# First stage of an attention and expert layer: rows normalised by VectorE, one f16 product for the keys' bias, other places for the setup's loads

## The chip, the cores and the metric

One core of one Trainium2 chip (trn2) runs the whole program. The metric is the device time of one execution in microseconds; the median of the runs counts. The profile is one further execution, taken by the hardware profiler.

## What is computed

The reference takes x of shape (2, 2048, 512) in f32, normalises each row over its 512 values, and gives x + attention(xn) + experts(xn):

```python
xn = _layernorm(x, axis=-1)
# attention, 16 heads of 32, latent size L = 128
c = jnp.einsum('bhsd,hld->bhsl', xh, Wdkv)
c = (c - mu) * jax.lax.rsqrt(var + 1e-05)
c = c * ln_g[None, :, None, :] + ln_b[None, :, None, :]
scores = jnp.einsum('bhsl,bhtl->bhst', q_lat, c) * (1.0 / np.sqrt(L))
w = jax.nn.softmax(where(mask, scores, -inf), axis=-1)
# experts: 8, the two with the highest gate logits, mean of relu(xn @ w + b)
x = x + attention(xn) + experts(xn)
```

The latent rows c are never formed. Since they are linear in a head's 32 values up to their scale, the setup folds `Wdkv`, `Wuk`, `Wuv`, `ln_g` and `ln_b` into 32x32 matrices per head. The variance of c comes from a quadratic form, keys and values from products of `xn * rs`, where `rs` is one over the deviation of c per row and head. The part of the keys that `ln_b` gives is a constant vector, the keys' bias.

## The kernel before

The program has four stages: setup with folding; the first stage, which makes queries, keys, values, gate logits and the f16 pieces of the normalised rows and stores them in DRAM; the attention per head; the experts and the last projection. The change touches the setup and the first stage.

The first stage works on 32 tiles of 128 rows, in chunks of four (CT = 4), the chunks of the two batches in turn, so eight chunks. Each engine has its own instruction list, in an order written out by hand, and waits on semaphores. In step p the tile at p gets its keys and values, the tile at p + 2 (QUERIES_AHEAD) its variance, queries and gate logits, the tile at p + 3 (TURN_AHEAD) is turned, and the tile at p + 4 (ROWS_AHEAD) is normalised. Statistics are read three tiles further ahead still (`means`, L785, L792). `run_tiles` (L264 to L273) runs the steps, four of them ahead of tile 0. Per step:

- **GpSimd** normalises the tile at p + 4 (L507: `(x - mean) * rs4`), subtracts its f16 half (L510, `xl_done`), and multiplies the tile at p + 2 by `rs` (L516, `xr_done`).
- **ScalarE** copies the turned `xr` of tile p (L666), makes the f16 half of the tile at p + 4 (L673, waits for `xn_done`), the queries' f16 half (L679), copies the turned tile p + 3 (L686), takes a square root (L693), makes the keys' f16 half (L699) and the values (L703). Once per chunk it takes the root of the four row variances (`spread`, L658).
- **VectorE** makes `rs4` once per chunk (L854), then `prod` and `var` for tile p + 2 (L861, L866), the queries' lower half (L868), the keys' lower half of tile p (L876), `rs` of tile p + 2 (L883), once per chunk the gates (L889 to L903), and then one or two row statistics (L785); none in one step of the four, and after the two of a chunk's end their means (L792).
- **TensorE** turns `xr` of tile p (L1095), forms the quadratic form (L1106), queries (L1112) and gate logits (L1119) of tile p + 2, turns tile p + 3 (L1130), and makes keys (L1139, L1140) and values (L1145) of tile p.
- **SP** issues all loads and stores of the stage. In the step of a chunk's tile 3 it waits for the keys' lower half (L379), stores keys, values (L383), rows (L390) and queries (L398), and in the next step loads x for the chunk after next into the same buffer (L372).

The keys' group is one f32 product and one f16 product with the bias for each of four blocks of 128 columns:

```python
t.matmul(PS[:, 5, k * P:(k + 1) * P], bdk[:, k, :], xrT[tl % 2][:, k, :], start=True, stop=False)
last = t.matmul(PS[:, 5, k * P:(k + 1) * P], bk_hl[0:HD + 1, k * P:(k + 1) * P], ones2[0:HD + 1, :],
                start=False, stop=True)
```

In the setup ScalarE issues the small loads and that of `expert_b` to all partitions (L643), waits for it, scales it by 1/2 (L646), and then copies the turned `Wo` (L651), from which TensorE makes the combined output matrix (L1077). VectorE reads the statistics of the first chunk (L785) and then takes the folded matrices out of PSUM (L815 to L821, `fold_done`, for which L1077 waits too), and goes on to the output matrix's lower half (L841) and the first `rs4` (L854).

## Time and profile before

| | |
|---|---|
| median of 3 runs | 1820.91 us (1818.5 to 1821.28) |
| profiled execution | 1804.26 us, its span 1802.5 us |
| busy: TensorE, VectorE, ScalarE, GpSimd | 1658.1, 1143.8, 969.2, 680.2 us |
| first normalisation starts | 49.84 us |
| last lower half of the keys ends | 290.5 us |
| first scores of the attention | 306.18 us |

The rows below are from the profiled execution; times are microseconds from the span's start unless marked ns. In a timeline a row is one instruction, or several of one kind in a row (x4), with start, duration, engine, line, operation, output and inputs with shapes; in brackets the time that the engine was idle before it and what ended that. A start with SPq or ACTq is a transfer being issued. PEclk is the granted share of TensorE's clock of 2.4 GHz. In these rows `arena` stands for many buffers: x, the normalised rows, queries, keys and values all lie in it.

### The profile page before, as it was taken

The page shows a single profiled execution, that of the slowest core. Times are in us where ns is not written, and L with a number is a line of the kernel's source. Part 1 is how long each engine was busy: PE and PEld are TensorE (multiplying, and loading weights), DVE is VectorE, ACT ScalarE, POOL GpSimd, SP SyncE. Part 2 cuts the span into 40 slices and gives each one's busy share as a digit, 9 for nine tenths or more (in the row PEclk, how much of TensorE's full clock was granted, in tenths as well). Part 3 has the DMA queues.
Part 4 walks back from the last instruction along what each step waited for, and adds up shares of the span by engine and source line. Part 5 has one row for each costly group of instructions (what it writes and reads, how often), then busy time and mean ns, then how long its engine had stood idle before and what let it go on. Part 6 is the DMA issues. An engine that isn't in the chain of part 4 may idle for free.

```text
span 1802.5 us, 46334 instructions
## 1 busy us (share of the span) xinstructions
PE 1658.1 (92%) x13408; PEld 940.8 (52%) x13409; DVE 1143.8 (63%) x2524; ACT 969.2 (54%) x1788; POOL 680.2 (38%) x1036
## 2 busy tenths in 40 slices
PE   4689885999999999999999999999999899998776
PEld 2567774455555555555555555555555355554333
DVE  3455556777777777777777777777777244444555
ACT  2455552566666666666666666666666533333332
POOL 1556550588222222322322322322222333332554
PEclk8899897899999999999999999999999899999998
DMA  5255645021020111111111112012111155554776
GB/s 144 94 172 181 186 142 166 8 61 30 30 59 29 29 49 39 29 37 51 29 29 59 29 29 59 29 29 59 29 29 36 55 173 174 170 174 148 234 236 221
DMA packets 126984, 160.87 MB, mean 89 GB/s; under 512 B 28352, under 2 KB 77504, under 8 KB 126816
## 3 DMA queue, kind: packets, MB, share of 16 engines
q1 hardware_dynamic: 108336, 121.15, 21.8%
q0 software_dynamic: 12992, 35.77, 7.2%
q10 hardware_dynamic: 5616, 3.45, 0.6%
q8 instruction: 21, 0.34, 0.1%
q14 instruction: 19, 0.16, 0.0%
HBM read 99.03 MB, written 61.15 MB: 89 GB/s over the span
## 4 chain that ended last, share of the span: by engine, by line
PE 68%; issue 8%; POOL 8%; DVE 8%; DMA 5%; ACT 2%; DVEq 0%; ACTq 0%; POOLq 0%; SPq 0%
PE PS L1213 26%; PE PS L1160 25%; PE PS L1264 10%; DMA arena<-expert_rows,cur 4%; POOL arena L507 4%; PE PS L1225 3%; DVE pm L971 3%; PE PS L1246 2%; POOL token_of_place L528 1%; POOL arena L510 1%; DVE arena L1034 1%; DMA eb_bc<-in_expert_b 1%; DVE arena L1035 1%; POOL arena L627 0%; ACT arena L686 0%
## 5 line engine op out<-in xcount | busy, mean ns | idle before, releaser
L971 DVE TENSOR_REDUCE pm<-PS 128x1 f32<-128x512 f32 (+3 forms) x1280 | 732.0, 603 | 279.9 <-PE PS L1160 273.3
L1160 PE MATMUL PS<-arena 96*64 96x512 f16 (+7 forms) x5120 | 723.0, 354 | 29.0 <-DVE PS L964 14.8
L726 ACT ACTIVATE arena<-PS 128x512 f32<-128x512 f32 (+1 forms) x1152 | 607.5, 574 | 258.5 <-PE PS L1160 255.1
L1213 PE MATMUL PS<-arena 128*33 128x512 f32 (+3 forms) x2560 | 660.1, 532 | 0.7 <-POOL arena L539 0.7
L1160 PEld LDWEIGHTS PS<-arena 96*64 96x64 f16 (+1 forms) x5120 | 354.4, 110 | 352.3 <-issue 141.5
L539 POOL TENSOR_SCALAR_AFFINE_SELECT arena<-arena 128x256 f32<-128x256 f32 (+1 forms) x256 | 111.0, 434 | 403.0 <-ACT arena L726 399.6
L1213 PEld LDWEIGHTS PS<-arena 128*33 128x33 f32 x2560 | 173.7, 112 | 83.7 <-POOL arena L539 2.8
L1160 PE MATMUL PS<-later,deny 128*64 128x128 f16 x1024 | 175.1, 223 | 0.0
L1264 PE MATMUL PS<-w_hi,arena 128*128 x576 | 172.9, 382 | 0.3 <-issue 0.3
L743 ACT ACTIVATE arena<-PS 128x1024 f16<-128x1024 f32 x72 | 73.7, 1024 | 151.3 <-PE PS L1246 151.3
L554 POOL TENSOR_TENSOR arena<-bv_bc,rden 128x128 f32 (+1 forms) x128 | 51.1, 399 | 236.5 <-DVE rden L984 236.0
L1011 DVE SCALAR_TENSOR_TENSOR arena<-PS,eb_bc 128x512 f32<-128x512 f32 x72 | 49.8, 692 | 127.8 <-PE PS L1264 127.8
L1160 PEld LDWEIGHTS PS<-later,deny 128*64 128x64 f16 x1024 | 92.5, 112 | 51.8 <-issue 24.8
L1264 PE MATMUL PS<-w_lo,arena 128*128 x288 | 110.0, 382 | 0.0
L719 ACT ACTIVATE turn<-PS 128x264 f32<-128x264 f32 x128 | 49.9, 390 | 102.4 <-PE PS L1225 102.4
L1296 PE MATMUL PS<-comb_hl,arena 128*128 128x512 f16 x384 | 96.5, 406 | 0.4 <-ACT arena L761 0.4
L547 POOL TENSOR_TENSOR bv_bc<-turn 128x132 f32<-128x132 f32 x128 | 53.1, 415 | 105.1 <-ACT turn L719 105.0
L733 ACT ACTIVATE arena<-PS 97x512 f32<-97x512 f32 x128 | 76.5, 598 | 27.6 <-PE PS L1213 27.6
L507 POOL TENSOR_SCALAR arena<-arena,mv,rs 128x512 f32<-128x512 f32 x32 | 66.3, 2073 | 51.9 <-DVE rs L854 51.9
L761 ACT ACTIVATE arena<-PS 128x1024 f16<-128x1024 f32 x32 | 32.8, 1024 | 96.1 <-PE PS L1283 96.1
L627 POOL DMA_INDIRECT arena<-expert_rows,cur x64 | 67.7, 1058 | 36.4 <-POOL cur L622 26.0
L1264 PEld LDWEIGHTS PS<-w_hi,arena 128*128 128x128 f16 x576 | 53.6, 98 | 52.7 <-issue 2.2
(177 smaller groups left out, 1690.0 us busy)
## 6 DMA issues: line engine op xcount, KB each, us to landing
expert_rows<-arena SPq DMA_DIRECT2D x72, 256.0 KB, 2.0
arena<-q_pieces SPq DMA_DIRECT2D x96, 128.0 KB
arena<-k_pieces SPq DMA_DIRECT2D x96, 128.0 KB
v_rows<-arena SPq DMA_DIRECT2D x8, 1056.0 KB, 6.4
arena<-v_rows SPq DMA_DIRECT2D x32, 264.0 KB
arena<-in_x SPq DMA_DIRECT2D x8, 1024.0 KB, 7.3
xn_rows<-arena SPq DMA_DIRECT2D x16, 512.0 KB, 4.3
q_pieces<-arena SPq DMA_DIRECT2D x32, 256.0 KB, 4.5
```

The lines of the kernel that those rows point to most:

```text
L507: g.tensor_scalar(xn[:, tl, :], x_in[u][:, tl, :], mv[:, u, tl, 0:1], rs4[:, u, tl:tl + 1], ALU.subtract, ALU.mult).then_inc(s["xn_done"], 1)
L539: g.affine_select(out=both[:, :, 0:wm], in_=both[:, :, 0:wm], compare_op=ALU.is_ge, fill=nought, base=0, pattern=[[step, 2], [1, wm]], cha ...
L627: g.indirect_dma_start(out=y_g[u][k], out_offset=None, in_=y_dram, in_offset=bass.IndirectOffsetOnAxis(ap=cur[:, TOP * u + k:TOP * u + k + ...
L726: a.activation(probs[kk % 4][:, a_ * CH:a_ * CH + w], PS[:, s2_bank(k, x), 0:w], ACT.Exp, scale=SCALE).then_inc(s["exp_done"], 1)
L733: a.activation(ot[q % 2][0:2 * HD + V1, :], PS[0:2 * HD + V1, 6 + q % 2, :], ACT.Copy).then_inc(s["ot_done"], 1)
L743: a.activation(xg_T[u].rearrange("p z k c -> p (z k c)"), PS[:, 4 + 2 * u:6 + 2 * u, :].rearrange("p z c -> p (z c)"), ACT.Copy).then_inc( ...
L971: v.reduce_max(pm[:, c, r, p:p + 1], PS[:, S1_BANK[n], 0:w], AX).then_inc(s["s1_done"], 1)
L1160: last = t.matmul(PS[h:h + P // 2, bank, cols], lhsT[:, h:h + P // 2], rhs, start=start, stop=stop)
L1213: last = t.matmul(PS[rows_, 6 + c % 2, CH - wds[a]:CH], v_sb[pu % 2][:, j + a, :], probs[pk % 4][:, a * off:a * off + wds[a]], start=p_ in ...
L1225: last = t.transpose(PS[:, 6 + q % 2, r * P:r * P + W_], ot[q % 2][0:W_, r * P:(r + 1) * P], ident[0:W_, 0:W_])
L1264: last = t.matmul(PS[:, u, :], xg_T[u][:, z, k, :], w[:, ds(e, 1), k * E:(k + 1) * E].rearrange("p e c -> p (e c)"), start=q_ == 0, stop=q ...
L1296: last = t.matmul(PS[:, u, :], oT[u][:, z, k, :], comb_hl[:, y, k, :], start=q_ == 0, stop=q_ == len(terms) - 1)
```

## The change

Three things change. VectorE instead of GpSimd normalises the rows, ahead of `prod` in each step, and the means no longer wait for the rows of the chunk before. The keys' bias is one f16 product of 512 columns, issued before the four f32 products; its operands are 98 rows high, with each block's two halves of the bias at partitions 0, 32, 64 and 96, and a matrix of ones and zeros that picks them. In the setup the load of `expert_b` is issued behind the output matrix's copies and has a semaphore of its own, its scaling comes after the first stage, and the means of the first chunk come behind the folding.

```diff
 # GpSimd, step
                 at = ahead_tile(i, p, ROWS_AHEAD, more)
                 if at:
                     n, u, tl, ii = at
-                    if tl == 0:
-                        pool.wait_ge(s["rs4_done"], count(ii * B + u + 1))
-                    pool.wait_ge(s["xr_done"], count(n - CT + 1))
-                    pool.sem_inc(s["row_from"], 1)
-                    g.tensor_scalar(xn[:, tl, :], x_in[u][:, tl, :], mv[:, u, tl, 0:1], rs4[:, u, tl:tl + 1],
-                                    ALU.subtract, ALU.mult).then_inc(s["xn_done"], 1)
                     pool.wait_ge(s["xh_done"], count(n + 1))
 # ScalarE
-            act.dma_start(eb_bc[:], expert_b.partition_broadcast(P)).then_inc(s["bias_in"], 16)
-            act.wait_ge(s["bias_in"], count(32))
-
-            a.activation(eb_bc[:].rearrange("p e c -> p (e c)"), eb_bc[:].rearrange("p e c -> p (e c)"), ACT.Copy,
-                         scale=1.0 / TOP).then_inc(s["eb_done"], 1)
-
...
+            act.dma_start(eb_bc[:], expert_b.partition_broadcast(P)).then_inc(s["eb_in"], 16)
             spread(0, 0)
             run_tiles(act, step)
+
+            act.wait_ge(s["eb_in"], count(16))
+            a.activation(eb_bc[:].rearrange("p e c -> p (e c)"), eb_bc[:].rearrange("p e c -> p (e c)"), ACT.Copy,
+                         scale=1.0 / TOP).then_inc(s["eb_done"], 1)
 # VectorE, means and setup
                 v.drain()
-                dve.wait_ge(s["xn_done"], count((ii * B + u - 1) * CT))
-                dve.sem_inc(s["aggr_at"], 1)
                 for t in range(CT):
...
-            means(0, 0, range(CT))
             dve.wait_ge(s["fold_ps"], count(1))
...
-            link(v.tensor_copy(bk_hl[0:HD + 1, :], PS[0:HD + 1, 4, :]))
-            link(v.tensor_tensor(bk_hl[HD:HD + 1, :], PS[HD:HD + 1, 4, :], bk_hl[HD:HD + 1, :], ALU.subtract))
-            link(v.memset(ones2[:], 0.0))
-            for r in (0, HD):
-                v.memset(ones2[r:r + 1, :], 1.0)
+            v.memset(bk_rows, 0.0)
+            link(v.memset(bk_pick, 0.0))
+            for k in range(KB):
+                r, c = slice(P // KB * k, P // KB * k + 2), slice(P * k, P * (k + 1))
+                v.memset(bk_pick[r, c], 1.0)
+                link(v.tensor_copy(bk_rows[r, :], PS[r, 4, c]))
+                r = slice(P // KB * k, P // KB * k + 1)
+                v.tensor_tensor(bk_rows[r, :], PS[r, 4, c], bk_rows[r, :], ALU.subtract)
             v.tensor_copy(bv_bc[:], PS[:, 5, :]).then_inc(s["fold_done"], 1)
 
+            means(0, 0, range(CT))
 # VectorE, step
                 if at and at[2] == 0:
                     n, u, tl, ii = at
+                    lnk, cnt = linker(dve, s["dve_rows"], ii * B + u)
                     dve.wait_ge(s["sd4_done"], count(ii * B + u + 1))
-                    v.reciprocal(rs4[:, u, :], sd4[:]).then_inc(s["rs4_done"], 1)
+                    lnk(v.reciprocal(rs4[:, u, :], sd4[:]))
+                if at:
+                    n, u, tl, ii = at
+                    dve.wait_ge(s["xr_done"], count(n - CT + 1))
+                    v.tensor_scalar(xn[:, tl, :], x_in[u][:, tl, :], mv[:, u, tl, 0:1], rs4[:, u, tl:tl + 1],
+                                    ALU.subtract, ALU.mult).then_inc(s["xn_done"], 1)
 # TensorE, step
+                    pe.wait_ge(s["kl_done"], count(n))
+                    R_ = P - P // KB + 2
+                    t.matmul(PS[:, 5, :], bk_rows[0:R_, :], bk_pick[0:R_, :], start=True, stop=False)
                     pe.wait_ge(s["xrt_done"], count(n + 1))
-                    pe.wait_ge(s["kl_done"], count(n))
                     for k in range(KB):
-                        t.matmul(PS[:, 5, k * P:(k + 1) * P], bdk[:, k, :], xrT[tl % 2][:, k, :], start=True, stop=False)
-                        last = t.matmul(PS[:, 5, k * P:(k + 1) * P], bk_hl[0:HD + 1, k * P:(k + 1) * P], ones2[0:HD + 1, :],
-                                        start=False, stop=True)
+                        last = t.matmul(PS[:, 5, k * P:(k + 1) * P], bdk[:, k, :], xrT[tl % 2][:, k, :], start=False, stop=k == KB - 1)
```

What moves on VectorE shows best in the step behind the gates, in the loop of the first stage. Before, one statistic (of a tile seven ahead) is followed at once by `prod`, the product with the quadratic form (waits `y_ps` from TensorE):

```order
L785 BN_STATS stats<-arena 128x6 [waits x_in0]
L859 REGISTER_ALU
L861 TENSOR_TENSOR arena<-PS,arena 128x512 [waits sd_done,y_ps]
L866 TENSOR_REDUCE var<-arena 128x16 [waits prod_done]
L868 SCALAR_TENSOR_TENSOR arena<-PS,arena 128x4x128 [waits qh_done]
L876 TENSOR_TENSOR arena<-PS,arena 128x4x128 [waits kh_done]
L883 RECIPROCAL rs<-sd 128x16 [waits xr_done,sd_done]
```

In the changed kernel the same stretch of VectorE has the normalisation between them:

```order
L778 BN_STATS stats<-arena 128x6 [waits x_in0]
L853 TENSOR_SCALAR arena<-arena,mv,rs 128x512 [waits xr_done]
L859 REGISTER_ALU
L861 TENSOR_TENSOR arena<-PS,arena 128x512 [waits sd_done,y_ps]
L866 TENSOR_REDUCE var<-arena 128x16 [waits prod_done]
L868 SCALAR_TENSOR_TENSOR arena<-PS,arena 128x4x128 [waits qh_done]
L876 TENSOR_TENSOR arena<-PS,arena 128x4x128 [waits kh_done]
L883 RECIPROCAL rs<-sd 128x16 [waits xr_done,sd_done]
```

The normalisation stands behind a statistic that waits for a load of x, and ahead of `prod`, `var` and both lower halves.

At a chunk's border the changed VectorE has this, from `rs` to the normalisation of the next chunk's first tile (the ISA rows are the sequencer's):

```order
L883 RECIPROCAL rs<-sd 128x16 [waits xr_done,sd_done]
L778 BN_STATS stats<-arena 128x6 x2
L783 BN_AGGR mv<-stats 128x2 x4
L848 ISA
L849 RECIPROCAL rs<-sd 128x4 [waits sd4_done]
L852 ISA [waits dve_rows]
L853 TENSOR_SCALAR arena<-arena,mv,rs 128x512 [waits xr_done]
```

The means have no wait for `xn_done` any more, and the normalisation waits for VectorE's own `rs4`.

## Rows read from the trace of the kernel before

**Rows 1.** Chain that ended last, to 420 us: start, duration, what
```profile
49.84 2.08 POOL arena L507
...
71.13 2.07 POOL arena L507
...
245.51 2.07 POOL arena L507
```

**Rows 2.** Timeline of one tile's ring, and the stage's last lower half
```profile
143.13 2.07 POOL L507 TENSOR_SCALAR arena<-arena,mv,rs 128x512 f32<-128x512 f32 x1
...
145.23 0.63 ACT L673 ACTIVATE arena<-arena 128x512 f16<-128x512 f32 x1 [2.51 <-POOL arena L507]
...
148.59 0.24 DVE L883 RECIPROCAL rs<-sd 128x16 f32<-128x16 f32 x1
...
148.91 1.05 POOL L516 TENSOR_TENSOR arena<-arena,rs 128x512 f32<-128x512 f32 x1 [1.80 <-DVE rs L883]
...
289.84 0.69 DVE L876 TENSOR_TENSOR arena<-PS,arena 128x512 f16<-128x512 f32 x1 [3.95 <-ACT arena L699]
```

**Rows 3.** Timeline of TensorE, one step: keys' group, values' group, next turn, next keys
```profile
138.17 0.44 PE L1139 MATMUL PS<-arena 128*128 128x128 f32 x2
...
140.43 1.16 PE L1145 MATMUL PS<-arena 128*128 128x128 f32 x8
141.43 0.60 PE L1095 MATMUL PS<-ident,arena 128*128 128x128 f32 x4
...
143.85 0.44 PE L1139 MATMUL PS<-arena 128*128 128x128 f32 x2
```

**Rows 4.** Groups of instructions by form: count | busy us, mean ns | idle before
```profile
L1296 PE MATMUL PS<-comb_hl,arena 128*128 128x512 f16 x384 | 96.5, 406 | 0.4 <-ACT arena L761 0.4
...
L828 DVE TENSOR_SCALAR arena<-arena 128x512 f32<-128x512 f32 x1 | 0.4, 416 | 0.0
```

**Rows 5.** Timeline of VectorE between `rs` and `prod`, border and gates
```profile
126.20 0.24 DVE L883 RECIPROCAL rs<-sd 128x16 f32<-128x16 f32 x1
...
128.79 0.69 DVE L861 TENSOR_TENSOR arena<-PS,arena 128x512 f32<-128x512 f32 x1
...
141.78 0.24 DVE L883 RECIPROCAL rs<-sd 128x16 f32<-128x16 f32 x1
...
144.35 0.70 DVE L785 BATCH_NORM_STATS2 stats<-arena 128x6 f32<-128x512 f32 x1
144.96 0.68 DVE L861 TENSOR_TENSOR arena<-PS,arena 128x512 f32<-128x512 f32 x1
```

**Rows 6.** Timeline of the attention, where VectorE and GpSimd meet
```profile
345.64 1.05 POOL L564 TENSOR_TENSOR w_hi<-x_g,ws_col 128x512 f16<-128x512 f32 x1
...
346.21 0.51 DVE L976 TENSOR_SCALAR mx<-mx 128x4 f16<-128x4 f32 x1
```

**Rows 7.** Timeline of SP at a chunk's border: keys' stores, load of x
```profile
126.31 0.92 SPq L379 DMA_DIRECT2D k_pieces<-arena  x2
...
133.73 0.61 SPq L372 DMA_DIRECT2D arena<-in_x  x1
```

**Rows 8.** Line L372, the six loads of x in the stage
```profile
DMA to landing us min/median/max: 5.7/7.0/7.5
```

**Rows 9.** Timeline of the setup
```profile
19.35 0.39 PE L1065 MATMUL PS<-arena 128*128 128x128 f32 x2
...
23.86 3.62 ACT L646 ACTIVATE eb_bc<-eb_bc 128x4096 f32<-128x4096 f32 x1 [12.09 <-DMA eb_bc<-in_expert_b]
...
26.94 2.47 DVE L785 BATCH_NORM_STATS2 stats<-arena 128x6 f32<-128x512 f32 x4 [11.12 <-DMA arena<-in_x]
...
29.89 3.55 DVE L815 TENSOR_SCALAR arena<-PS 32x128 f32<-32x128 f32 x12
...
49.40 0.18 DVE L854 RECIPROCAL rs<-sd 128x4 f32<-128x4 f32 x1
```

**Rows 10.** Stretch of 5 us: busy us per engine (instructions), PEclk, DMA share, GB/s
```profile
130.00:135.00 5.00, 5.00 (x20) 3.97 (x20) 1.75 (x4) 2.76 (x6) 2.34 (x3) 0.51 1.05 317
```

More of the change, by code:

```diff
@@ L72, in layer_kernel @@
         ident16 = sb("ident16", [P, P], f16)
-        ones2 = sb("ones2", [HD + 1, P], f16)
         gw_hl = sb("gw_hl", [P, KB, 2, NE], f16)
@@ L127, in layer_kernel @@
         q_hi, q_lo, k_hi, k_lo = (tA(KB * CH, f16).rearrange("p (k s) -> p k s", k=KB) for _ in range(4))
-        bk_hl = tA(E, f16)
         v_st = [tA(CT * H * V1).rearrange("p (h t f) -> p h t f", t=CT, h=H) for _ in range(2)]
+        bk_rows = tA(P, f16)
+        bk_pick = tA(KB * P, f16)
         tA = carve(arena1)
@@ L192, in layer_kernel @@
         s = {n: sem(n) for n in (
-            "eb_done w_in wqo_in g_in wo_in gate_in bias_in boc_done bob_ps bob_done zeroed consts wc_ps wc_done gw_done fold_ps fold_done bk_ps bk_done bv_ps bv_done "
+            "eb_in eb_done w_in wqo_in g_in wo_in gate_in bias_in boc_done bob_ps bob_done zeroed consts wc_ps wc_done gw_done fold_ps fold_done bk_ps bk_done bv_ps bv_done "
             "wot_ps wot_done comb_ps comb_hi comb_done gates_done dve0 "
-            "bd_done x_in0 x_in1 stage_in scaled stage_free pool_link mv_done sd4_done rs4_done xn_done xh_done xl_done tp_ps "
-            "row_from aggr_at xt_done y_ps q_ps g_ps prod_done var_done sd_done rs_done xr_done tr2_ps xrt_done qh_done ql_done "
+            "bd_done x_in0 x_in1 stage_in scaled stage_free pool_link mv_done sd4_done xn_done xh_done xl_done tp_ps "
+            "xt_done y_ps q_ps g_ps prod_done var_done sd_done rs_done xr_done tr2_ps xrt_done qh_done ql_done "
             "k_ps kh_done kl_done vv_ps v_done lg_done dve_rows dve_gates x_out0 x_out1 q_out0 q_out1 k_out0 k_out1 v_out0 v_out1 "
@@ L832, in _ @@
             v.tensor_tensor(bdq_hl[:, 1], bdq, bdq_hl[:, 0], ALU.subtract).then_inc(s["bd_done"], 1)
-            dve.wait_ge(s["bias_in"], count(32))
+            dve.wait_ge(s["bias_in"], count(16))
             link(v.tensor_scalar(bo_bc[:], bo_bc[:], 1.0 / TOP, None, ALU.mult))
```

## The prediction

> **What bounds the kernel now.** All of the change lies before 291 us, in the setup and the first stage, so I read the chain of waits there first: it gives the pace. The first row tile is normalised (L507) at 49.84 us, that of the second chunk at 71.13, that of the eighth and last at 245.51, and the last lower key half (L876) ends at 290.5 [rows 1, 2]. Six chunks of four tiles take 174.4 us, 29.1 each; what comes before the first of them takes 21.3, what follows the last 45.0. The timeline of one tile shows why it is not faster [rows 2]: a ring that runs through four engines. GpSimd normalises a tile (2.07 us from 143.13), ScalarE had stood idle for it 2.51 us and starts the f16 half at 145.23; behind that in ScalarE's fixed order are the queries' half, the turned tile, the square root and the keys' half; VectorE then makes the keys' lower half and at 148.59 the reciprocal `rs`; GpSimd scales with it (1.05 us from 148.91), and only then normalises the next tile. That is 6.81 us a tile at best. TensorE is no part of it but is near: its step is 5.68 us at full clock, of which the keys' group takes 2.26 and the values' 1.00 [rows 3].
>
> **Normalisation on VectorE.** GpSimd loses 32 instructions of 2.07 us, and L516 no longer has one behind it. VectorE gets 32. No row has a TENSOR_SCALAR with two per-partition operands there. The nearest, L828, same shape and f32 from SBUF, takes 0.42 us [rows 4]; the upper bound is 0.69, what the other 512-column instructions of VectorE take (L876 [rows 2]). I take 0.42.
>
> The new ring, piece by piece. From the end of normalisation to the start of `rs`: 145.20 to 148.59, 3.39 us [rows 2]. From `rs` to the next normalisation VectorE does, in its fixed order, one of four things [rows 5]:
> - tile with nothing between: at most the 0.24 of `rs`; VectorE's instructions overlap a little (the statistic of 144.35 is shown with 0.70, and the next starts after 0.61), so I take 0.16;
> - one row statistic: 0.16 + 0.56, 0.72 (0.56 for 0.61, an estimate);
> - two statistics, their means, ScalarE's root, `rs4`: 126.20 to 128.79, 2.6;
> - the gates and one statistic: 141.78 to 144.96, 3.2.
>
> A chunk has each once: 4 x (3.39 + 0.42) + 0.16 + 0.72 + 2.6 + 3.2 = 21.9 us (0.2 more with the longer values). The wait of the means for the previous chunk's rows falls away and costs nothing either way: VectorE has issued those itself.
>
> **GpSimd and VectorE in each other's way.** The trace has a case: L976, a TENSOR_SCALAR out of SBUF, with four elements a partition, takes 0.51 us, more than L828 with 512, when it starts at 346.21 beside L564 of GpSimd, and it ends at 346.72, just behind GpSimd's 346.69 [rows 6]. So a normalisation that meets a GpSimd instruction will end 0.03 to 0.45 us behind it; I take 0.3, since the start of an instruction passes in the shadow as that of L976 did, and its data don't. After `rs` (0.24) GpSimd starts its 1.05 at once; with one statistic between, VectorE comes to the normalisation while it runs, and ends at 0.24 + 0.08 + 1.05 + 0.3 = 1.67 after `rs` instead of 1.14: +0.5. In the other three cases GpSimd has finished or VectorE is first. Chunk: 22.4. The Trainium skill (SBUF - State Buffer, Who interferes with whom) says that a VectorE instruction in a two-port mode and a GpSimd instruction exclude each other for their whole length; by it the whole 0.42 would follow, 0.1 us more per chunk. The rows show less, and I keep the rows.
>
> **The x load.** Here a cover goes. SP stores keys, values, rows and queries and only then issues the load of the chunk after next: 126.31 for the keys of tile 3, 133.73 for the load, so 7.4 us later, and it lands 5.7 to 7.5 us on, 7.0 in the middle [rows 7, 8]. Data are there 14.4 us (13.1 to 14.9) after the keys' lower half of tile 3. Their first statistic runs just ahead of the `prod` at 144.96, from about 144.4, 18 us after it, so nothing waits now. In the new ring it would come due after 2.6 + 0.42 + 3.39 + 0.16 + 0.42 + 3.39 + 2.6 (3.2 less the statistic) - 0.1 = 12.9 us. VectorE then waits 1.5 us for it, and the chunk takes 23.9. Of the six intervals five have such a load behind them: 6 x 22.4 + 5 x 1.5 = 141.9, against 174.4: **-32.5**. The bounds: no wait and no meeting with GpSimd, 6 x 21.9, is -43; at 14.9 -30.
>
> **The bias product.** Four f16 products between the f32 ones go, one of 512 columns comes. The values' group, four f32 pairs of the same shape with nothing between, takes 1.00 [rows 3]; the 512-column f16 product is nearest to L1296, 96.5 us for 384, 0.25 each [rows 4]. Keys' group 1.25 instead of 2.26, TensorE's step 4.67, 18.7 a chunk, below 23.9. So within the chunks it is worth nothing; at the end, where no rows are normalised and the steps follow TensorE, it counts.
>
> **Before and after the six chunks.** Lead-in, 21.3 now: the first three tiles are normalised in one go instead of 4 us apart, so I let the first `prod` come 3 us earlier, at 6 for 9 (an estimate). From there some 3.4 to `rs`, then 0.72 + 0.42 + 3.39 + 2.6: 10.5 and 6 are 16.5: **-5**. End, 45.0 now: three normalised tiles at 6.81 or more (20.6) become 3.97, 6.4 (gates) and 3.97, 14.3, -6.3; the four remaining steps each lose 1.0 of the keys' group: together **-10**.
>
> **Setup.** Today ScalarE stands waiting for `expert_b` until 23.86 and scales it for 3.6 us before it copies the turned `Wo`, and VectorE waits for x before the folding: L815 starts at 29.89, while its products end at 19.74 [rows 9]. Both waits go. The folding starts 9.9 earlier; its small instructions grow: four times a memset, a cast and a subtraction of 128 columns, estimated by L815's 0.28 (3.55 for 12 of 128 columns) and 0.17 for a memset as 3.7 in all against 2.1, so +1.6. What follows, up to `rs4` at 49.40, comes 8.3 earlier: **-8.3**. The means of the first chunk now stand behind the folding, at 28; x landed at 27 with `expert_b` ahead of it, so they don't wait, and end before TensorE's next products do. The load of `expert_b` (2 MB) now runs at 36 us beside nothing, its scaling at the stage's end, where ScalarE's next work is the first softmax, behind the routing of VectorE and the first scores. I cost both at nothing; without that cover it would be 3.6 us.
>
> **Sum:** -8.3 - 5 - 32.5 - 10 = -56. The profiled execution took 1804.3 us (span 1802.5), so 1748 for one like it. It was 0.9% below the median of the runs; the forecast for the median is 1820.9 - 56 = **1765 us**. The later stages only start earlier.
>
> **The rivals.**
> - *Everything hidden fits (18%).* The load lands in 12.9 us, since the transfers wait less for each other, or VectorE is never held. For it: the load alone needs 5.7 to 7.5. Against: SP issues the stores first and the burst stays as large. Chunk 21.9: 11 us less, 1754.
> - *TensorE's clock becomes the bound (22%).* After the wait at a chunk's border the granted clock is 0.51, at the 1.2 GHz level, through 130 to 135 us [rows 10]. Now that hits nobody. A chunk is 18.7 of work at full clock; one such stretch of about 5.7 us adds 2.85, the border's wait 2.2: 23.8, just what I forecast. Two stretches give 26.6, 2.7 x 6 = 16 more: 1781.
> - *Less comes of it (11%).* The normalisation takes 0.69, the f32 products stay at the 0.44 us a pair that they have between the f16 ones [rows 3], or the setup has another wait: up to 10 more, 1775. It is also the case in which the change doesn't do what it says: if a pair costs that without the f16 ones, the keys' group is 1.9 and only 0.3 is saved.
> - *Slower (2%).* The x load decides: each microsecond that it lands later costs 5, since VectorE holds back `prod` and through it everything. From 14.4 + 56 / 5 = 25.6 us the gain is gone. At 28, should the stores of the faster chunk pile up on one queue, +12: 1833. Against it: the one load issued behind a whole burst lands 7.0 us later and the next burst begins only at tile 1, with the load long down.
> - *As forecast (47%).* 1757 to 1773.
>
> **The numbers.** The range takes the fast rival, the forecast and most of the TensorE one: 1750 to 1784. About 0.2% is what a measurement can tell here, 3.6 us. Only the last rival and some unseen wait in a later stage reach that: faster 0.96, same 0.015, slower 0.025.
>
> **What would show it.** The chain from tile to tile runs over VectorE, ScalarE and TensorE with no L507 of GpSimd; chunks of about 24 us; a VectorE wait for the x load of 1 to 2 us per chunk, on the first statistic; normalisations of 0.42 us, about 0.9 where L516's successor runs; the keys' group in 1.25 us; `rs4` first at 41 us. I am wrong on the mechanism if statistics never wait for x, or if TensorE has no idle time at the border; wrong on the size if chunks take under 22 or over 26 us. That stage two starts 56 us earlier and nothing else moves is the last test.

## The result and the profile after

| | before | changed kernel |
|---|---|---|
| median of the runs | 1821.10 us (1818.5 to 1823.49, 4 runs) | 1763.25 us (1759.39 to 1766.15, 4 runs) |
| ratio, with its 95% interval | | 0.9681 [0.9658, 0.9705] |
| profiled execution | 1804.26 us, span 1802.5 | 1764.17 us, span 1762.0 |
| first normalisation starts | 49.84 us | 41.11 us |
| first normalisations of chunks 1 and 2 apart (lead-in) | 21.3 us | 16.2 us |
| the six chunks that follow | 174.4 us, 29.1 each | 143.4 us, 23.9 each |
| from the last chunk's first normalisation to the last lower key half | 45.0 us | 32.3 us |
| last lower key half ends | 290.5 us | 233.0 us |
| first scores | 306.18 us | 248.66 us |
| busy: TensorE, VectorE, ScalarE, GpSimd | as in the table ahead | 1613.6, 1161.9, 967.6, 614.9 us |

So 57.8 us less, against a forecast of 56. The stage itself ends 57.5 us earlier; the two spans are only 40.5 apart, since heads 0 to 3 of the attention took longer in the second execution (75, 35, 35 and 33 us in the one, 81, 39, 41 and 34 in the other, counted from the stage's end to the start of GpSimd's last product of each head, L554 before and L548 after; everything behind them agrees within 0.4). Both kernels have that difference, as the runs below show: it goes with the batch of runs (the three batches below ran on three chips). Comparisons here are therefore between kernels of one batch, or of the first stage alone, which ended within 0.4 us in the three profiles in which it is that of the kernel before (290.53, 290.85 and, on the third chip, 290.80).

One chunk of the changed kernel, from the timeline of VectorE, GpSimd, SP and TensorE (start, duration, engine, line, operation, output and inputs with shapes; in brackets the idle time and what ended it). It answers to [rows 2, 5, 7]:

```profile
119.96 0.24 DVE L883 RECIPROCAL rs<-sd 128x16 f32<-128x16 f32 x1
120.12 0.63 DVE L778 BATCH_NORM_STATS2 stats<-arena 128x6 f32<-128x512 f32 x1
120.28 1.05 POOL L510 TENSOR_TENSOR arena<-arena,rs 128x512 f32<-128x512 f32 x1 [1.81 <-DVE rs L883]
120.67 0.94 DVE L853 TENSOR_SCALAR arena<-arena,mv,rs 128x512 f32<-128x512 f32 x1
...
124.38 0.69 DVE L876 TENSOR_TENSOR arena<-PS,arena 128x512 f16<-128x512 f32 x1 [0.86 <-ACT arena L687]
124.99 0.24 DVE L883 RECIPROCAL rs<-sd 128x16 f32<-128x16 f32 x1
125.10 0.92 SPq L379 DMA_DIRECT2D k_pieces<-arena  x2
...
127.57 0.55 DVE L853 TENSOR_SCALAR arena<-arena,mv,rs 128x512 f32<-128x512 f32 x1
127.75 1.16 PE L1141 MATMUL PS<-arena 128*128 128x128 f32 x8 [1.65 <-ACT arena L654]
...
131.66 0.24 DVE L883 RECIPROCAL rs<-sd 128x16 f32<-128x16 f32 x1
131.82 0.46 DVE L853 TENSOR_SCALAR arena<-arena,mv,rs 128x512 f32<-128x512 f32 x1
131.98 1.20 POOL L510 TENSOR_TENSOR arena<-arena,rs 128x512 f32<-128x512 f32 x1 [1.81 <-DVE rs L883]
132.08 1.13 SPq L372 DMA_DIRECT2D arena<-in_x  x1
...
135.79 0.24 DVE L883 RECIPROCAL rs<-sd 128x16 f32<-128x16 f32 x1
...
139.37 0.69 DVE L778 BATCH_NORM_STATS2 stats<-arena 128x6 f32<-128x512 f32 x1 [1.14 <-DMA arena<-in_x]
139.97 0.53 DVE L853 TENSOR_SCALAR arena<-arena,mv,rs 128x512 f32<-128x512 f32 x1
```

The ring can be walked down these rows. From `rs` at 119.96 over the statistic to the normalisation's end, 1.65 us (forecast 1.67); from there to the next `rs`, 3.38 (3.39); over the border to the next normalisation, 2.58 (2.6); with nothing between, 0.16 (0.16). At the gates 4.18, of which 1.14 is the wait for the load of x (3.2 with its statistic, and a wait of 1.5, were forecast). The keys of tile 3 are stored at 125.10, the load goes out at 132.08 and lands at 139.34.

Waits of the first stage (engine, output and line, what they waited for: us in total, times, the longest), and the landing of the loads of x, line L372:

```profile
ACT arena L661 <- DVE arena L853: 50.6, 30, 5.8
```

```profile
  DVE stats L778: 7.1, 5
...
DMA to landing us min/median/max: 6.1/7.0/8.0
```

VectorE waited five times for x, 7.1 us in all, 1.4 on average (0.91 to 2.49): one wait per chunk, on the statistic behind the gates, as the prediction had it. ScalarE now waits for VectorE where it waited for GpSimd.

The chain that ended last, between two normalisations (start, duration, what):

```profile
120.75 0.87 DVE arena L853
...
124.38 0.70 DVE arena L876
...
127.05 2.18 SPq L390
...
129.42 1.11 SPq L398
...
132.08 7.26 DMA arena<-in_x
...
139.97 0.54 DVE arena L853
```

No normalisation on GpSimd is left in it. From the lower key half of tile 3 on, the chain runs through SP's stores of rows (L390) and queries (L398) to the load, and back to VectorE: in this execution the load's place in SP's order sets the pace behind each border.

The setup and the end, which answer to [rows 9] and to the last of [rows 2]:

```profile
20.31 3.59 DVE L805 TENSOR_SCALAR arena<-PS 32x128 f32<-32x128 f32 x12 [5.63 <-PE PS L1065]
...
28.50 2.47 DVE L778 BATCH_NORM_STATS2 stats<-arena 128x6 f32<-128x512 f32 x4
...
40.89 0.18 DVE L849 RECIPROCAL rs<-sd 128x4 f32<-128x4 f32 x1
41.11 1.00 DVE L853 TENSOR_SCALAR arena<-arena,mv,rs 128x512 f32<-128x512 f32 x2
...
233.08 3.60 ACT L702 ACTIVATE eb_bc<-eb_bc 128x4096 f32<-128x4096 f32 x1
```

The folding starts at 20.31, `rs4` is there at 40.89, and the scaling of `expert_b` lies at 233.08, where VectorE's routing covers it (the first scores are 15.6 us away). The granted clock, in stretches of 5 us (busy us per engine with instructions, then PEclk, DMA share and GB/s), against [rows 10]:

```profile
123.00:128.00 5.00, 2.92 (x46) 2.35 (x45) 3.56 (x11) 2.63 (x6) 1.56 (x2) 1.00 0.39 108
```

TensorE stands idle at this border too (2.92 of 5 us busy), yet the clock stays at its 2.4 GHz level. It was at 0.51 behind the border in the kernel before. This isn't so in the whole stage, nor in every execution. In this profile the clock did fall twice, behind the two last waits for x (2.49 and 1.38 us), while TensorE worked again:

```profile
169.00:172.00 3.00, 3.00 (x29) 2.91 (x28) 2.97 (x7) 1.65 (x4) 1.63 (x2) 0.50 0.00 0
```

So it was again from 193 to 195. The two steps in which it fell first are as long there, 4.62 and 6.90 us from one normalisation to the next (165.11, 169.73, 176.63), as in a chunk without it. The second profile of this kernel, below, has more of it.

### The profile page after: what moved, and what is told of

Read it like the earlier page. It is cut to its first block, busy times and chain, and to the rows that moved or that the text cites. A ratio compares the mean times of both kernels' runs of the same rounds, so it can differ in the third digit from the quotient of the medians.

```text
span 1762.0 us, 46067 instructions
## 1 busy us (share of the span) xinstructions
PE 1613.6 (92%) x13312; PEld 909.6 (52%) x13313; DVE 1161.9 (66%) x2565; ACT 967.6 (55%) x1788; POOL 614.9 (35%) x1004
## 4 chain that ended last, share of the span: by engine, by line
PE 74%; DVE 9%; DMA 6%; issue 4%; ACT 2%; SPq 2%; POOL 1%; DVEq 0%; POOLq 0%; ACTq 0%
PE PS L1213 29%; PE PS L1160 27%; PE PS L1264 11%; PE PS L1225 3%; DMA arena<-expert_rows,cur 3%; DVE pm L971 3%; DMA arena<-in_x 2%; PE PS L1246 2%; DVE arena L1034 1%; SPq L398 1%; DVE arena L853 1%; SPq L390 1%; DVE arena L1035 1%; DVE mx L976 1%; ACT arena L667 1%
## 5 line engine op out<-in xcount | busy, mean ns | idle before, releaser
L548 POOL TENSOR_TENSOR arena<-bv_bc,rden 128x128 f32 (+1 forms) x128 | 51.0, 399 | 243.5 <-DVE rden L984 243.1
L1225 PEld LDWEIGHTS PS<-ident,arena 97*128 97x128 f32 x512 | 47.1, 140 | 59.9 <-ACT arena L726 32.4
```

The lines of the kernel that those rows point to most:

```text
L1225: last = t.transpose(PS[:, 6 + q % 2, r * P:r * P + W_], ot[q % 2][0:W_, r * P:(r + 1) * P], ident[0:W_, 0:W_])
```

## The experiments

Lengths by stage, in us, each from the kernel's profiled execution. "Chunk" is the mean of the six; the last column is the time of heads 0 to 3. Chip 1 and the batch of the result have the longer heads, chips 2 and 3 the shorter, as has the profile of the kernel before with its 178.

| kernel | chip | first norm. | lead-in | chunk | end | stage ends | heads 0 to 3 |
|---|---|---|---|---|---|---|---|
| before again | 1 | 50.16 | 21.3 | 29.06 | 45.0 | 290.85 | 194 |
| normalisation alone | 1 | 47.83 | 16.1 | 24.62 | 42.6 | 254.28 | 197 |
| bias product alone | 1 | 50.57 | 21.3 | 28.97 | 41.2 | 286.92 | 195 |
| setup alone | 1 | 39.17 | 21.3 | 29.07 | 45.0 | 279.86 | 197 |
| load first | 2 | 40.42 | 16.0 | 22.83 | 32.3 | 225.71 | 178 |
| statistics earlier | 2 | 41.33 | 14.8 | 25.91 | 33.2 | 244.78 | 178 |
| both | 2 | 41.21 | 14.8 | 20.13 | 33.2 | 209.94 | 178 |
| change, no scaling | 2 | 41.56 | 16.3 | 24.03 | 32.3 | 234.32 | 176 |
| change again | 3 | 40.78 | 16.4 | 23.70 | 32.3 | 231.65 | 178 |
| before, no scaling | 3 | 50.00 | 21.3 | 29.08 | 45.0 | 290.80 | 174 |
| all | 3 | 41.47 | 16.2 | 20.14 | 33.2 | 211.65 | 176 |
| change, no scaling, again | 3 | 40.85 | 16.1 | 23.84 | 32.3 | 232.29 | 175 |

The kernel before took 1821.32 us beside the first four, 1804.40 beside the second four and 1803.01 beside the last.

### The kernel before, once more

> The kernel before, unchanged, with a profile of its own. In the two profiles at hand the stage up to the end of the last L876 got 57.5 us shorter (290.5 to 233.0) but the span only 40.5: the first three heads take 39.1, 41.1 and 33.7 us with the change and 34.9, 34.9, 33.2 before. Theory A: the profiled execution of before was a lucky one; usual ones lose the same 17 us in the first heads (VectorE's L976 held by GpSimd's identifier writes and weight splits), so this profile shows a span near 1819 and heads of 39 to 41 us. Theory B: the change itself brings the loss; then this profile shows 1802 and heads of 34.9, and the medians' 58 us are an accident. Timed: ratio 1.000 by both.

1820.80 us, ratio 0.9997 [0.9987, 1.0007], and a profiled execution with a span of 1819.4 where the one at hand has 1802.5. Its first stage is the same to 0.3 us (290.85 for 290.53). Of the 16.9 us between the spans 15.7 sit in heads 0 to 3 (194.1 for 178.4). The kernel before has the long heads too, so the change didn't make them.

### Each part alone

The normalisation by VectorE without the others (in part; the means lose their wait, as in the change):

```diff
-                    g.tensor_scalar(xn[:, tl, :], x_in[u][:, tl, :], mv[:, u, tl, 0:1], rs4[:, u, tl:tl + 1],
-                                    ALU.subtract, ALU.mult).then_inc(s["xn_done"], 1)
...
+                    dve.wait_ge(s["xr_done"], count(n - CT + 1))
+                    v.tensor_scalar(xn[:, tl, :], x_in[u][:, tl, :], mv[:, u, tl, 0:1], rs4[:, u, tl:tl + 1],
+                                    ALU.subtract, ALU.mult).then_inc(s["xn_done"], 1)
```

> Only the normalisation moves to VectorE; bias product and setup as before. My theory (the ring bounds, TensorE is covered): TensorE's chunk is 4 x 5.68 = 22.7 us, just under ring and x load, so chunks of about 24.2 instead of 29.1, lead-in -5, end -6: 40 to 44 us less, 1777 to 1781. Rival (TensorE bounds with a cold stretch per chunk): chunks of 26 to 27, 25 to 30 us less, 1791 to 1796.

1788.11 us, 0.9817 [0.9801, 0.9833]: 33.2 us less, between the two ranges, so neither theory has it. The chunk of 24.62 is nearer to the first (24.2), and the end is what it missed: -2.4 for -6. The timeline of TensorE, the keys' group (L1137 with the bias between, L1138), and its waits:

```profile
131.12 0.44 PE L1137 MATMUL PS<-arena 128*128 128x128 f32 x2
131.50 0.23 PE L1138 MATMUL PS<-ones,arena 33*128 33x128 f16 x1
...
138.01 0.49 PE L1137 MATMUL PS<-arena 128*128 128x128 f32 x2 [1.05 <-ACT arena L660]
```

```profile
PEld PS L1137 <- ACT arena L660: 10.0, 8, 1.6
```

Windows of the loop and of the end (busy us of TensorE first):

```profile
60.00:230.00 170.00, 160.88 (x1773) 138.65 (x1773) 124.61 (x349) 109.71 (x203) 63.50 (x57) 0.98 0.67 202
...
90.00:92.00 2.00, 2.00 (x8) 1.66 (x9) 0.98 (x2) 1.55 (x3) 0.59 (x1) 0.50 1.07 297
166.00:168.00 2.00, 2.00 (x16) 1.94 (x15) 0.60 (x3) 1.16 (x3) 1.12 (x1) 0.50 1.04 345
...
246.00:250.00 4.00, 3.86 (x18) 3.08 (x17) 0.71 (x2) 1.30 (x3) 0.00 (x0) 0.61 0.65 183
```

Here VectorE never waits for x inside the loop. TensorE is busy 160.9 of 170 us: the ring has run into it. Four steps of 5.68 are 22.7, the border's wait for ScalarE's turned copy (L660) adds 1.1 to 1.6: 24.0, as three of the six chunks are. The two in which the clock fell to its 1.2 GHz level behind the border, from 90 and from 166 us, are 25.5 and 25.9, and the mean is 24.6. So the rival of the expectation is nearer in its mechanism, TensorE as the bound, with two stretches of slow clock instead of six. The end, at 42.6, hardly shrinks: the last four lower halves come 21.5 us behind that of tile 27 where they took 18.9 before and 14.15 in the changed kernel, partly because the clock fell to 0.61 from 246 to 250 us.

The bias product alone:

```diff
-                        t.matmul(PS[:, 5, k * P:(k + 1) * P], bdk[:, k, :], xrT[tl % 2][:, k, :], start=True, stop=False)
-                        last = t.matmul(PS[:, 5, k * P:(k + 1) * P], bk_hl[0:HD + 1, k * P:(k + 1) * P], ones2[0:HD + 1, :],
-                                        start=False, stop=True)
+                        last = t.matmul(PS[:, 5, k * P:(k + 1) * P], bdk[:, k, :], xrT[tl % 2][:, k, :], start=False, stop=k == KB - 1)
```

> Only the keys' bias as one product of 512 columns. My theory: keys' group 2.26 to 1.25 us, but the ring through GpSimd hides it; only the four last steps gain 1 us each and the setup loses 1.6: 0 to 4 us less, 1817 to 1821. Rival (the keys' group is on the path of every tile, through k_hi and k_lo): 32 x 1.0 us less, 1789.

1815.15 us, 0.9969 [0.9957, 0.9982]: 6.2 us less, above the 0 to 4 expected. The chunks stay at 29.0, and the end loses 3.8: what the prediction said of a product in cover. The stage ends 3.9 us earlier, as the first theory has it; the other 2.3 us came behind it, without a named cause.

The setup alone (in part; the means of the first chunk stand behind the folding, as in the change):

```diff
-            act.wait_ge(s["bias_in"], count(32))
...
+            act.dma_start(eb_bc[:], expert_b.partition_broadcast(P)).then_inc(s["eb_in"], 16)
             spread(0, 0)
             run_tiles(act, step)
+
+            act.wait_ge(s["eb_in"], count(16))
...
```

> Only the setup's loads and the means of the first chunk in their new places. My theory: first normalisation 8 to 10 us earlier (no small bias instructions added, so rather 10), everything behind it moves along, 8 to 10 us less: 1811 to 1813. Rival: part of it is lost because the 2 MB load of expert_b now runs beside the first chunk's stores, 3 to 5 us less only, 1816 to 1818.

1812.10 us, 0.9945 [0.9928, 0.9961]: 9.2 us less, as expected. The first normalisation comes 11.0 us earlier, and all chunks stay as they were.

The three measured gains add up to 48.6 us, the change took 57.8. By stage: the starts add to 12.9 us less (11.0 and 2.3, less 0.4) against 9.05 together; lead-in, chunks and end add to 38.7 against 48.8. So about 10 us exist only when normalisation and bias product are both there: 3.7 in the chunks (27.3 apart, 31.0 together) and 6.5 at the end (6.2 apart, 12.7 together).

### The load's place, and the statistics' place

Load first: SP loads x in the step in which the chunk before has been normalised, ahead of the stores of tile 3 (in part; the last steps are written out, so that no load too many is issued).

```diff
-                at = ahead_tile(i, p, ROWS_AHEAD - 1, more)
-                if at and at[2] == CT - 1 and more:
+                at = ahead_tile(i, p, ROWS_AHEAD, more)
+                if at and at[2] == CT - 1 and (load if p == PER_IT - 1 else more):
```

> The changed kernel, with SP issuing the load of x as soon as the chunk's last tile is normalised, ahead of the four kinds of stores instead of behind them. My theory: the load's landing is the last wait of each chunk and costs VectorE 1 to 2.5 us there, 7.1 in all; with it gone chunks of 22.5 to 22.9 instead of 23.9 (the second chunk, which has its load early, shows 22.8): 6 to 8 us less, 1755 to 1757. Rival (TensorE's cold stretch bounds the chunk): chunks stay at 23.5 to 24, 0 to 2 us less.

1741.01 us, 0.9651 [0.9635, 0.9667], by the ratios 5.5 us under the changed kernel. The chunk is 22.83, against 23.9 and 23.7 with the late load, and VectorE never waits for x in the stage. SP's queue at the border:

```profile
119.73 0.40 SPq L372 DMA_DIRECT2D arena<-in_x  x1
...
123.03 0.92 SPq L379 DMA_DIRECT2D k_pieces<-arena  x2
```

The load goes out 3.3 us before the keys of tile 3 instead of 7 us behind, and lands after 5.1 to 5.7 us. The stage is 7.3 us shorter than in the changed kernel's first profile, about its 7.1 us of waiting, and 5.9 shorter than in its second. There the waits for x are only four and 2.2 us in all, and yet its chunks take 23.70. The rest goes with TensorE's clock, lower behind five borders of that profile, and VectorE waits five times for TensorE, 2.3 us in all (windows; in the timeline VectorE's `prod`):

```profile
105.00:110.00 5.00, 5.00 (x54) 4.99 (x53) 3.35 (x8) 4.00 (x9) 2.35 (x3) 0.71 1.05 317
...
109.27 0.69 DVE L861 TENSOR_TENSOR arena<-PS,arena 128x512 f32<-128x512 f32 x1 [0.68 <-PE PS L1106]
```

VectorE's next statistic starts at 115.40, where in the first profile it waits for x until 115.43: one limit lies in the other's cover. With the load first the one chunk with a fallen clock (0.50 from 104 to 106 us) takes 23.53 and the others 22.56 to 22.80. So moving the load removed its wait, and the second profile shows that the place of the load is not the only thing that holds a chunk at 23.7.

Statistics earlier: the row statistics stand ahead of the keys' lower half, where VectorE waits for ScalarE anyway.

```diff
+                at = ahead_tile(i, p, ROWS_AHEAD + 3, more)
+                if at and at[2] < CT - 1:
+                    means(at[1], at[3], (at[2],) if at[2] < CT - 2 else (CT - 2, CT - 1))
                 at = ahead_tile(i, p, 0, more)
                 if at:
                     dve.wait_ge(s["kh_done"], count(n + 1))
```

> The changed kernel with the row statistics and the means moved on VectorE from behind rs to behind the queries' lower half, where VectorE idles about 0.9 us a tile; so the normalisation stands directly behind rs. My theory: the meetings with GpSimd's L510 go (all normalisations 0.45 to 0.55 us, none at 0.94 to 1.02) and the ring alone would give 19 to 20 us a chunk, but the load of x still lands 14.4 us behind the keys' lower half of tile 3 and some 9 us of ring follow it: chunks of 23 to 24, only 0 to 6 us less, 1757 to 1763, and the wait for the load grows to 3 to 5 us a chunk. Rival (the ring bounds, the load is no limit): chunks of 20, 24 us less, 1739.

1755.00 us, 0.9724 [0.9708, 0.9741]: worse than the change, where 0 to 6 us less were expected. VectorE and line L372:

```profile
117.52 0.69 DVE L778 BATCH_NORM_STATS2 stats<-arena 128x6 f32<-128x512 f32 x1 [6.91 <-DMA arena<-in_x]
```

```profile
  DVE stats L778: 34.3, 5
...
DMA to landing us min/median/max: 6.8/7.2/7.4
```

The five waits grew from 7.1 to 34.3 us. The first chunk, which waits for no load, is 19.7; the others are 26.8 to 27.4, that is 19.7, a wait of 6.2 to 7.5 and 0.3 to 0.9 more; the granted clock is at 0.50 behind these waits (118 to 124 us), which may be the rest. The edit was right for the ring and wrong for the load, and the forecast had counted the first and too little of the second: the statistic comes due 5.6 us earlier (7.6 us behind the keys' lower half of tile 3, where the changed kernel has 13.2) while the landing stays 14.5 us behind it.

Both edits together:

> Both moves: load of x ahead of the stores, statistics behind the queries' lower half. My theory: neither limit is left, the ring gives 19 to 20 us a chunk with TensorE's 18.7 just below: 22 to 28 us less than the changed kernel, 1735 to 1741. Rival (TensorE, or the transfers, which need 17 us a chunk, bound first): chunks of 21.5 to 23, 8 to 14 us less, 1749 to 1755.

1723.57 us, 0.9553 [0.9537, 0.9569]. Chunks of 20.13, no wait for x in the loop, and a granted clock of 1.00: the first theory. Two edits of which one alone gives 6 to 7 us of the stage and the other alone costs 12 to 13 (8 by the ratios of the timed runs, 0.9724 to 0.9682; its profiled execution was the slowest of its four) are worth 22 to 23 together (233.0 or 231.65 to 209.94).

### The scaling of the largest scores

In the attention, L976 scales 128x4 largest scores to f16. It can go if the reduction writes f16 and the stationary row is -1 instead of -64 (`MS` is 64; the -128 of a later expectation is a slip):

```diff
-                    lnk(v.reduce_max(mx[:, c, :], pm[:, c, :, :], AX))
-                    lnk(v.tensor_scalar(mx16[:, c, 0:CT], mx[:, c, :], 1.0 / MS, None, ALU.mult))
+                    lnk(v.reduce_max(mx16[:, c, 0:CT], pm[:, c, :, :], AX))
```

> The changed kernel without the instruction L976 in the attention: the row maxima are written as f16 by the reduction, unscaled, and the keys' extra row holds -1 instead of -64. All four usual profiles of this stage lose 17 us in heads 0 to 3 against the lucky one. My theory: L976 is held up to 1.5 us by GpSimd's identifier writes and weight splits, and this disturbs the order of the first heads; without it heads 1 to 3 go to 34 to 35 us and 15 to 20 us are gained, 1743 to 1748. Rival (the identifier writes cost GpSimd's own chain, masks and sums come late): heads stay at 39 to 41, 0 to 3 us gained.

1741.11 us, 0.9643 [0.9627, 0.9659]: by the ratios 7 us under the changed kernel, in the range of neither theory. It ran on a chip with short heads, where it could not settle what makes them long on the other.

> The changed kernel once more, to see it beside the kernel before in one batch whose profiled executions can be compared with each other. The stage until the last lower key half ends at 233.0 us as in its first profile, whatever the later heads take. Theory A (a chip has its own time for heads 0 to 3, the same for every kernel): the ratio is that of the medians so far, 0.968, whether this batch has the kernel before at 1804 or at 1821 us, so 57 to 58 us less. Theory B (the change itself made heads 0 to 2 longer, 81 for 75 us and 39 for 35, as its first profile shows beside that of the kernel before): where the kernel before runs at 1804 us it takes 1761 to 1764, 41 to 43 us less.

1745.47 us, 0.9682 [0.9665, 0.9698], beside 1803.01 for the kernel before: 57.5 us less, as in the batch with the long heads. Theory A holds. The change did not lengthen heads 0 to 2; in this profile they take 74.9, 35.0 and 35.0.

> The kernel before with one part of the attention altered: the largest score of a row is written in f16 at once by the reduction, and the scaling of 128x4 values behind it (L976) is left out, the row of the stationary operand it is multiplied with set to -1 instead of -128. Theory A (on chips where the kernel before takes 1821 us, L976 is what makes heads 0 to 2 longer: it is held up to 1.5 us behind pairs of GpSimd instructions): there heads 0 to 3 fall from some 81, 41, 38, 34 us to 75, 35, 35, 33, and the total to 1800 or less. Theory B (those heads are longer for another reason, a transfer or the clock): the total falls by only the 4 to 7 us that the changed kernel lost by the same edit. Where the kernel before takes 1804 us both give 1797 to 1800.

1795.12 us, 0.9957 [0.9943, 0.9972]: 7.9 less, a little more than the 4 to 7 that both theories gave for this chip (1797 to 1800), so it doesn't choose between them.

> The changed kernel without the scaling of the largest scores, again, for its ratio to the changed kernel in one batch. On a chip with 1804 us: 1739 to 1743, some 5 us under the changed kernel if heads 0 to 3 depend on the chip alone. On a chip with 1821 us: 1741 if L976 held behind GpSimd is the cause of the longer heads, 1756 to 1759 if it is not.

1737.35 us, 0.9636 [0.9620, 0.9652]: 8.1 less than the changed kernel in the same batch. So the edit is worth the same 8 us with and without the change, where 5 were expected. By the profiles 3 of the 8 come in heads 0 to 3 (178.0 to 175.0), the rest behind them.

> The changed kernel with all three edits: load of x in its own step, statistics ahead of the keys' lower half, and no scaling of the largest scores (its stationary row -1). If the parts are independent: the kernel of the two first edits took 80.8 us less than the kernel before, and the last edit was worth another 4 to 7 on a chip with 1804 us, so 1717 there. On a chip with 1821 us theory A of the kernel before without the scaling gives 1717 too, theory B 1733. If the scaling hides behind something in this kernel, nothing is gained over the ratio of 0.955.

1716.54 us, 0.9517 [0.9501, 0.9533]: 86.5 us less than the kernel before and 28.9 less than the change. The two first edits gave 80.8 on the second chip, so the third adds 5.7 here and not 8: the sum of the parts is 2.4 us more than the whole.

What stays open is why heads 0 to 2 take some 15 to 18 us longer in the two batches near 1821 us. There the profiles show this (changed kernel, first profile; GpSimd's rows beside):

```profile
289.39 1.01 POOL L522 DMA_INDIRECT token_of_place<-token_id,place_at  x1 [0.17 <-issue]
...
289.95 1.56 DVE L976 TENSOR_SCALAR mx<-mx 128x4 f16<-128x4 f32 x1
...
290.42 1.06 POOL L560 TENSOR_TENSOR x_g<-x_g,ws_col 128x512 f32<-128x512 f32 x1
```

and in the kernel's second profile, on the third chip:

```profile
286.33 1.05 POOL L558 TENSOR_TENSOR w_hi<-x_g,ws_col 128x512 f16<-128x512 f32 x1
286.89 0.52 DVE L976 TENSOR_SCALAR mx<-mx 128x4 f16<-128x4 f32 x1
```

L976 meets two GpSimd instructions in a row and ends 0.03 us behind the second (291.51 for 291.48) in the one; in the other it meets one. That is a candidate for part of it, and only that: the kernel without L976 never ran where the heads are long, so whether it is cause or consequence isn't shown.

## Why the prediction came out as it did

- **Setup, -8.3 forecast, -8.7 measured** (49.84 to 41.11). The folding starts at 20.31 where its products end, and nothing waits for `expert_b` or x. The scaling costs nothing at its new place: from the stage's end to the first scores it is 15.7 us in both kernels. Right, with the pieces -9.6 (forecast -9.9) for the folding's start and +1.8 (forecast +1.6) for the bias rows, 3.87 us from the folding's end to the copy behind them against 2.09; the last 0.9 lie behind them. Alone the setup's part gives 11.0: it has the 1.8 of the bias rows less, and its folding started 0.85 us sooner in its profile (19.46).
- **Lead-in, -5 and -5.1.** Right.
- **The six chunks, -32.5 and -31.0.** 23.90 a chunk for 23.65 forecast on average. The ring piece by piece, the meeting with GpSimd and the wait for x came out within a tenth or two. Two sizes were off and offset each other: the normalisation takes 0.46 with nothing between and 0.53 to 0.55 elsewhere, not 0.42 as L828; and the wait is 1.4, not 1.5. In the second profile the same sum, 23.7, has other terms: 2.2 us of waiting for x and 2.3 for TensorE in the stage. The prediction had priced the forecast at 23.9 and its rival of the clock at 23.8, so the length of a chunk can't tell them apart; that it fits both profiles is in part luck.
- **The bias product "within the chunks is worth nothing".** This step failed. It compared TensorE's new chunk (4 x 4.67 = 18.7) with the new ring, and never the old chunk of TensorE (4 x 5.68 = 22.7, and the border's wait) with it. The part with the normalisation alone shows that 24.6 would have come out: the product is worth 4.3 us in the chunks, though alone it gives none there. The total was right because both were in the change.
- **The product's own size.** A keys' group of 1.25 us was forecast, 0.25 for the product and 1.00 for eight f32 products. The timeline of TensorE in the changed kernel has the group from the product at 132.39 to the values' at 133.50, 1.11 us:

```profile
132.39 0.38 PE L1138 MATMUL PS<-arena 98*128 98x512 f16 x1
...
132.61 1.05 PE L1141 MATMUL PS<-arena 128*128 128x128 f32 x8
...
133.50 1.06 PE L1145 MATMUL PS<-arena 128*128 128x128 f32 x8
```

  The steps of 4.43 stand in the chain at the stage's end (values at 216.77 and 221.20). So 0.22 and 0.89. The case that f32 products keep their 0.44 a pair is refuted: two of them cost 0.22 without an f16 one between. Whether the change of type or the single open group makes it wasn't tried.
- **The end, -10 forecast, -12.7 measured.** This is the term that was mis-sized. The three tiles of the ring gave 6.4 for the 6.3 expected (20.6 to 14.2). The piece from the start of the last normalisation to the lower half of tile 27, 5.5 before and 3.9 now, had been left out: -1.6, which is that normalisation's own duration, 2.07 to 0.46; behind it both kernels take 3.47. The four steps after it give -4.7 (18.9 to 14.15), not -4, the last two 1.4 each (4.65 to 3.23).

- **The sum**: -8.7 - 5.1 - 31.0 - 12.7 = -57.5 in the profiled executions, and the medians say -57.8 and, on another chip, -57.5.
- **"It was 0.9% below the median of the runs".** The prediction took the difference of 17 us between profile and median as a part of the time that both kernels share, and set the sum against the median. That held. It did not know what the difference was, and that it didn't matter is luck. It was no single lucky execution: the batch of 1804.40 has seven runs of the kernel before from 1802.09 to 1805.8. It goes with the batch and its chip; on which chip the profile of the kernel before was taken isn't on record.
- **The rivals.** Everything hidden fits: refuted by five waits for x; but its chunk of 21.9 can nearly be had, 22.8, by moving the load. TensorE's clock: it acts in part. In the first profile it fell behind two borders and lengthened no step; in the second it fell behind five, made VectorE wait for `prod` (0.68 us at 109.27) and ran largely in the cover of the load of x; in the variant with the normalisation alone it made two chunks 1.5 and 1.9 us longer than the 24.0 of the others. The 26.6 us a chunk that the rival priced never came. Slower through the load: the landing was 14.3 us behind the lower half of tile 3 (125.07 to 139.34), far from 25.6. How strong that lever is shows where the statistics come earlier: waits of 6.9 instead of 1.4 made the later chunks 27.1 instead of 23.9, although the ring there is 3 us shorter (19.7 for 22.8 in the first chunk).

## What to carry to other kernels

When a ring through several engines gets shorter, put every other period beside the new length, in their old form too: the next engine's step, and the time from the last use of a buffer over the queue of stores to its reload. A part that is worth 6 us alone can be worth 10 more beside another, and an edit that speeds the ring can lose 8 until the load that it uncovers is moved, so test such edits in pairs. Look at a second profile of the same kernel before a wait is called the bound: here the waits for x were 7.1 us in one and 2.2 in the other, with the same time. Compare kernels within one batch on one chip, and by stages: here a stage that the change doesn't touch differed by some 17 us between batches.

## What was not expected of the hardware

- **A normalisation on VectorE that meets a running GpSimd product ends 0.28 us behind it, whenever it starts.** L853 ends 0.28 us behind L510 (121.61 and 121.33 above), and again in the same kernel (145.62 and 145.34), as in all seven such meetings with L510 in this profile:

```profile
144.60 1.02 DVE L853 TENSOR_SCALAR arena<-arena,mv,rs 128x512 f32<-128x512 f32 x1
```

```profile
144.29 1.05 POOL L510 TENSOR_TENSOR arena<-arena,rs 128x512 f32<-128x512 f32 x1 [1.89 <-DVE rs L883]
```

  The Trainium skill (SBUF - State Buffer, Who interferes with whom) has a VectorE instruction in a two-port mode and a GpSimd one exclude each other for the whole instruction; by it, as an estimate, the 0.46 to 0.55 that the normalisation takes alone would follow behind GpSimd. The rows show less: about half of the instruction hides. The other way round, with VectorE first at 131.82, GpSimd's instruction takes 1.20 instead of 1.05. There VectorE was 0.16 us ahead. With 0.09 us it is too little: in the kernel with the statistics earlier VectorE starts first and still ends 0.28 us behind.

```profile
211.61 1.42 DVE L853 TENSOR_SCALAR arena<-arena,mv,rs 128x512 f32<-128x512 f32 x1
211.70 1.05 POOL L510 TENSOR_TENSOR arena<-arena,rs 128x512 f32<-128x512 f32 x1 [3.01 <-DVE rs L886]
```

- **The same kernel takes 1821 us in a batch on one chip and 1803 to 1804 in batches on two others**, each repeatable within its batch, with nearly all of the difference (15.7 of 16.9 us) in one stretch of 178 or 194 us in which VectorE, GpSimd and transfers interleave, and with TensorE's granted clock the same over the span (0.962 in both profiles of the kernel before). Each chip had one batch, so whether the chip or something else about the batch makes it isn't shown.
